# Third cross attention: the value product as two diagonal blocks of 64 columns

## The chip, the cores and the metric

The kernel runs on one core of a Trainium2 chip. The metric is device time in microseconds (us). A core has TensorE (in profile rows PE for matmuls, PEld for the loading of weights), VectorE (DVE), ScalarE (ACT), GpSimd (POOL) and SyncE (SP, which issues most DMAs). They meet through semaphores.

## The reference, cut to what matters

The model has twelve layers: four rounds of cross attention, self attention and a feed-forward layer, on 8 batches of 64 tokens with 256 channels. The change is in the third round's cross attention. It has 16 heads of 64 channels, 64 latents a batch, and 1601 context rows plus the 64 latents themselves as keys.

```python
xn, ln_lat = layer_norm(x, g1, b1), layer_norm(latents, g2, b2)
q = ln_lat @ Wq
k, v = jnp.split(jnp.concatenate([xn, ln_lat], axis=1) @ Wkv, 2, axis=-1)
...                                   # to 16 heads of 64
weight = softmax(mask(q * scale @ (k * scale).T))
out = einsum('bhln,bhnd->bhld', weight, v)
return out_as_rows @ Wout
```

## The kernel before, in words

`layer_2_xattn` (from line 3770) doesn't make keys and values of every head. It takes the key weights into the queries, and it weighs the normed context rows themselves: for each head the softmax weights times the rows give a mean row of 256 channels, and only that mean is multiplied with the head's value weights.

The work goes in 64 units: 8 batches (`b`) by 8 pairs of heads (`r`); u = 8 b + r. The 128 partitions of a unit are 2 heads of the pair by 64 latents. TensorE does for each unit, in `unit` (line 4040):

- `scores(u + 2)`, float16 products in three terms (line 4009), two units ahead of their use.
- sometimes a `prepare` group for a later batch (lines 3981, 3986, 3994).
- 13 products of the weights' high half with both halves of the rows, 512 columns each, into PSUM bank `ACC` (line 4055). Ahead of the one with m = 4 it calls `turn_means(u - 1)`, which transposes the mean rows of the unit before (line 4017).
- 13 products of the weights' low half with the rows' high half, 256 columns each (line 4060). Ahead of the one with m = 1 it calls `project(u - 1)`, the function that the change touches (line 4021).

`project` multiplies the pair's value weights `wv` (128 columns, 2 heads by 64 channels) with the turned means `meanT` (128 columns, 2 heads by 64 latents), in float32, summed over NC = 2 chunks of 128 channels, into bank 5. The result is 128 by 128: each head's value weights times each head's means. The two off-diagonal blocks mix one head's weights with the other's means. ScalarE's `keep_heads` (line 4160) takes only the diagonal ones, 64 by 64 each, to `oT`.

A float32 product appears in the records as two matmuls and two weight loads, so that the two calls in `project` are four records of each kind. The last unit's `project(63)` stands behind the loop, among the output products (line 4035).

Instructions stand in the order in which each engine's block issues them. TensorE's block takes waits on `post_read` (bank 5 is free) in `turn_means` and `project`. ScalarE turns meanT around between the two (`copy_means`).

Other places of the same kernel have products of 33 or 64 output columns, put to one of the two halves of the partitions: line 3431 (33 columns, first and last cross attention with heads of 16), line 912 (64 columns, 36 streamed), line 1284 (64 columns, 256 streamed, the halves in turn) and line 2789 (64 rows by 64 columns). Line 100 is `warm`, a full float16 product of 512 columns that holds no result.

Of the kernel before, what the change touches and what calls it, by code (L numbers as in the profile page):

```python
# [21 lines left out]
P = 128  # L22
B, S, D = 8, 64, 256
TOK = B * S
NT = TOK // P
NC = D // P
# [47 lines left out]
class Core:  # L74
# [19 lines left out]
    def sb(self, ctx, name, shape, dt=F32):  # L94
        return ctx.enter_context(self.nc.sbuf_tensor(name, shape, dt))
# [3674 lines left out]
def layer_2_xattn(k):  # L3770

    nc, PS, ins = k.nc, k.PS, k.ins
    DH = 64
# [12 lines left out]
    PREP, POST_BANK, ACC = (4, 6), 5, 7  # L3786
# [44 lines left out]
    with ExitStack() as c_:  # L3831
# [7 lines left out]
        wv = sb("wv", [P, NC, R * P])  # L3839
# [23 lines left out]
        meanT = sb("meanT", [P, NC, P])  # L3863
# [7 lines left out]
        with nc.Block() as block:  # L3871
# [100 lines left out]
            def _(pe):  # L3972
# [48 lines left out]
                def project(n):  # L4021
                    r = n % R
                    pe.wait_ge(post_read, 2 * n + 1)
                    for c in range(NC):
                        last = nc.tensor.matmul(PS[:, POST_BANK, 0:P], wv[:, c, r * P:(r + 1) * P], meanT[:, c, :],
                                                start=(c == 0), stop=(c == NC - 1))
                    last.then_inc(post_made, 1)

                def project_heads(t, heads):
# [10 lines left out]
                def unit(b, r):  # L4040
                    u = b * R + r
                    if u + 2 < U:
                        scores(u + 2)
                    for group, of in fills(b, r):
                        prepare(group, of)
                    if u == U - 2:
                        pe.wait_ge(prep_read, len(made_as))
                    if u + 2 >= U:
                        project_heads(u + 2 - U, range(R))
                    pe.wait_ge(high_turned, 16 * (u + 1))  # L4050
                    pe.wait_ge(sums_copied, u)
                    for m in range(KT):
                        if u > 0 and m == MEANS_AT:
                            turn_means(u - 1)
                        nc.tensor.matmul(PS[:, ACC, :], pth[:, u % 2, m, :], rows2[:, b % 2, :, :, m, :], start=(m == 0), stop=False)  # L4055
                    pe.wait_ge(low_turned, 16 * (u + 1))
                    for m in range(KT):
                        if u > 0 and m == VALUES_AT:
                            project(u - 1)
                        last = nc.tensor.matmul(PS[:, ACC, 0:D], ptl[:, u % 2, m, :], rows2[:, b % 2, 0, :, m, :], start=False,  # L4060
                                                stop=(m == KT - 1))
                    last.then_inc(sums_made, 1)
# [4 lines left out]
                for c in range(NC):  # L4067
                    last = nc.tensor.transpose(PS[:, FIRST_BANK, c * P:(c + 1) * P], lat[:, 0, c * P:(c + 1) * P], k.ident[:])
# [4 lines left out]
                for r in range(R):  # L4073
                    for j in range(NC):
                        last = nc.tensor.matmul(PS[:, Q_BANK, r * S:(r + 1) * S], wq[:, j, r * P:(r + 1) * P], latT[:, j, 0:S],
                                                start=(j == 0), stop=(j == NC - 1))
                last.then_inc(first_q, 1)
                pe.wait_ge(lat_scaled, NT)
                for c in range(NC):
                    for t in range(1, NT):  # L4080
                        last = nc.tensor.transpose(PS[:, LAT_BANK + c, t * P:(t + 1) * P], lat[:, t, c * P:(c + 1) * P], k.ident[:])
# [15 lines left out]
                pe.wait_ge(scored, U)  # L4097
                project_heads(3, range(R - 1))
                project(U - 1)
                project_heads(3, range(R - 1, R))  # L4100

# [355 lines left out]
```

## Time and profile before

| | |
|---|---|
| three runs, us | 2571.61 median, 2571.34 to 2571.94 |
| profiled execution, first to last instruction, us | 2561.7 |
| what lies around it, to the median of the runs, us | 9.9 |
| TensorE busy with matmuls | 2332.1 us, 91% |
| VectorE, ScalarE, GpSimd busy | 64%, 49%, 32% |

The profile has no total time of its own for the execution; the span from its first to its last instruction is compared with the median of the runs. A row of the timeline gives the start, and the time until the last of its records ends. Matmuls are pipelined: a record of 0.27 us does not hold TensorE for 0.27 us, and it is the distance between starts that counts. The shape `128*64 128x36 f32` is 128 rows and 64 columns of weights, 36 streamed columns in float32.

### The profile page before, as it was taken

To read this page: it belongs to the slowest core of one execution; us is meant where nothing else is said; L and a number is where in the kernel's file an instruction comes from. 1 tells how busy PE (TensorE), PEld (TensorE's weight loads), DVE (VectorE), ACT (ScalarE), POOL (GpSimd) and SP (SyncE) were. 2 spreads that over 40 slices of the span, in tenths; PEclk is the share of its full clock that TensorE was granted. 3 is DMA by queue.
4 is the path that set the end of the run, shared out by engine and by line. 5 is a ranking of instruction groups with operands and counts; after the bars stand their busy time and mean duration, and the time that the engine had idled before them with its cause. 6 is when DMAs were issued, how large, how long until landed. Compare 5 with 4: busy or idle time off the path is not lost. (4 is left out here: it accounts for less than half of the span.)

```text
span 2561.7 us, 44459 instructions
## 1 busy us (share of the span) xinstructions
PE 2332.1 (91%) x17354; PEld 1491.6 (58%) x17354; DVE 1651.5 (64%) x3198; ACT 1248.1 (49%) x2071; POOL 809.9 (32%) x660
## 2 busy tenths in 40 slices
PE   8885789999979889999999999699789999998898
PEld 6763556666654455656665666355456666666554
DVE  6976365555448756888888854654666666554577
ACT  3334145444444225555555553676345555554465
POOL 6610142242205202331233300055444454342253
PEclk9997899999999989999999999899999999999999
DMA  4202344233204047677776563133322222120221
GB/s 117 68 1 93 95 118 107 70 84 103 63 22 146 0 122 138 127 138 127 148 152 129 110 118 75 39 99 99 103 65 70 72 78 83 48 65 22 67 96 58
DMA packets 358593, 226.42 MB, mean 88 GB/s; under 512 B 289913, under 2 KB 326610, under 8 KB 358386
## 3 DMA queue, kind: packets, MB, share of 16 engines
q1 hardware_dynamic: 355314, 215.20, 34.5%
q0 software_dynamic: 3072, 8.39, 1.1%
q8 instruction: 139, 2.28, 0.4%
q14 instruction: 68, 0.56, 0.1%
HBM read 114.87 MB, written 0.52 MB: 45 GB/s over the span
## 5 line engine op out<-in xcount | busy, mean ns | idle before, releaser
L100 PE MATMUL PS<-hot 128*128 128x512 f16 x460 | 138.8, 439 | 82.4 <-DVE l0a_g L1119 17.5
L3951 POOL TENSOR_TENSOR l2x_rows<-l2x_rows,l2x_one 128x256 f16<-128x256 f32 (+1 forms) x91 | 90.9, 1025 | 378.9 <-DVE l2x_rows L1507 352.0
L4055 PE MATMUL PS<-l2x_rows,l2x_pth 128*128 128x512 f16 x832 | 200.4, 379 | 1.0 <-DVE l2x_mean L4264 0.9
L3709 DVE CUSTOM_DVE_ANT_0 l1x_junk<-PS,l1x_bias 128x1024 bf16<-128x1024 f32 (+1 forms) x128 | 123.3, 991 | 95.7 <-PE PS L3369 94.8
L4257 DVE TENSOR_TENSOR l2x_pl<-l2x_sc,l2x_ph 128x1664 f16<-128x1664 f32 x64 | 124.7, 1948 | 44.1 <-ACT l2x_ph L4134 43.4
L3709 DVE CUSTOM_DVE_ANT_0 l3x_junk<-PS,l3x_bias 128x1024 bf16<-128x1024 f32 (+1 forms) x128 | 123.6, 991 | 42.3 <-PE PS L3369 41.1
L4152 ACT ACTIVATE l2x_meanT<-PS 128x256 f32<-128x256 f32 x64 | 24.5, 383 | 250.0 <-PE PS L4017 250.0
L4242 DVE CUSTOM_DVE_ANT_0 l2x_sc<-PS,l2x_bias 128x1665 f32<-128x1665 f32 x64 | 120.9, 1889 | 38.2 <-issue 37.0
L3579 ACT ACTIVATE l3x_pT<-PS 128x512 f32<-128x512 f32 x144 | 84.5, 593 | 120.3 <-PE PS L3415 117.7
L100 PEld LDWEIGHTS PS<-hot 128*128 128x128 f16 x460 | 45.6, 109 | 154.0 <-issue 41.8
L4009 PE MATMUL PS<-l2x_kh,l2x_qth 128*128 128x512 f16 (+1 forms) x512 | 132.0, 339 | 1.5 <-issue 1.5
L4009 PE MATMUL PS<-l2x_kh,l2x_qtl 128*128 128x512 f16 (+1 forms) x512 | 132.0, 339 | 0.0
L4009 PE MATMUL PS<-l2x_kl,l2x_qth 128*128 128x512 f16 (+1 forms) x512 | 132.0, 339 | 0.0
L3579 ACT ACTIVATE l1x_pT<-PS 128x512 f32<-128x512 f32 x144 | 83.9, 594 | 88.3 <-PE PS L3415 87.8
L4055 PEld LDWEIGHTS PS<-l2x_rows,l2x_pth 128*128 128x128 f16 x832 | 79.3, 98 | 72.3 <-issue 2.6
L4127 ACT ACTIVATE l2x_sc<-l2x_sc,l2x_shift 128x1665 f32<-128x1665 f32 x64 | 107.9, 1686 | 19.5 <-DVE l2x_shift L4244 19.4
L4060 PE MATMUL PS<-l2x_rows,l2x_ptl 128*128 128x256 f16 x832 | 111.6, 273 | 0.0
L3431 PE MATMUL PS<-l1x_pT,l1x_v 128*33 128x128 f32 (+1 forms) x1664 | 110.9, 276 | 0.0
L3431 PE MATMUL PS<-l3x_pT,l3x_v 128*33 128x128 f32 (+1 forms) x1664 | 110.9, 276 | 0.0
L4134 ACT ACTIVATE l2x_ph<-l2x_sc 128x1664 f16<-128x1664 f32 x64 | 101.8, 1590 | 7.9 <-DMA l2x_pth<-l2x_ph 6.1
L3431 PEld LDWEIGHTS PS<-l3x_pT,l3x_v 128*33 128x33 f32 (+1 forms) x1664 | 83.4, 111 | 29.4 <-issue 20.1
L1642 POOL TENSOR_TENSOR l2f_unit_l<-l2f_unit,l2f_unit_h 128x384 f16<-128x384 f32 x72 | 74.6, 1058 | 70.9 <-ACT l2f_unit L1634 70.9
(867 smaller groups left out, 6231.0 us busy)
## 6 DMA issues: line engine op xcount, KB each, us to landing
l2f_unit<-in_L_ffn_units_dram SPq DMA_DIRECT2D x36, 384.0 KB, 3.0
l3f_unit<-in_L_ffn_units_dram SPq DMA_DIRECT2D x34, 384.0 KB, 2.9
l1x_kst<-l1x_kh SPq DMA_DIRECT2D x128, 100.1 KB, 2.2
l3x_kst<-l3x_kh SPq DMA_DIRECT2D x128, 100.1 KB, 2.2
l2x_rows<-in_ctx_dram SPq DMA_DIRECT2D x8, 1536.0 KB
l1x_ctx<-in_ctx_t_dram SPq DMA_DIRECT2D x7, 1601.0 KB, 7.3
l3x_ctx<-in_ctx_t_dram SPq DMA_DIRECT2D x7, 1601.0 KB, 6.6
l1x_kst<-l1x_kl SPq DMA_DIRECT2D x64, 100.1 KB, 2.2
```

The costliest lines, as they stand in the source:

```text
L100: self.nc.tensor.matmul(self.PS[:, bank, :], self.hot[:, 0:P], self.hot[:], start=True, stop=True)
L3431: last = nc.tensor.matmul(PS[at:at + VW, PV_BANK + b % 2, (u // 2) * P:(u // 2 + 1) * P], v33[0:n, b % 2, m, u, :], pT[0:n, (b * KT + m) % ...
L3579: nc.scalar.activation(to, of, ACT.Exp, scale=1.0 / S_SCALE).then_inc(exp_done, 1)
L3709: v.tensor_tensor_reduce(junk[:, slot(it), 0:n], slot_banks(it)[:, 0:n], bias[:, 0 if normed else b % 2, at:at + n], 1.0, LOWEST, ALU.add, ...
L3951: last = nc.gpsimd.tensor_tensor(high[:, at], of[:, at], one[0:p, at].unsqueeze(2).unsqueeze(3).to_broadcast([p, i, NC, P]), ALU.mult)
L4009: last = nc.tensor.matmul(PS[:, j, 0:n], x[:, d, r, :], y[:, b % 2, d, at:at + n], start=(e == 0), stop=(e == len(terms) - 1))
L4055: nc.tensor.matmul(PS[:, ACC, :], pth[:, u % 2, m, :], rows2[:, b % 2, :, :, m, :], start=(m == 0), stop=False)
L4060: last = nc.tensor.matmul(PS[:, ACC, 0:D], ptl[:, u % 2, m, :], rows2[:, b % 2, 0, :, m, :], start=False, stop=(m == KT - 1))
L4127: nc.scalar.activation(sc[:], sc[:], ACT.Exp, bias=shift[:, u % 2:u % 2 + 1], scale=1.0 / S_SCALE, accum_out=rsum[:, u % 4:u % 4 + 1]).the ...
L4134: nc.scalar.activation(ph[:], sc[:, 0:ODD], ACT.Copy).then_inc(p_high, 1)
L4242: link(v.tensor_tensor_reduce(sc[:], PS[:, 0:len(cols), :].rearrange("p b n -> p (b n)")[:, 0:KEYS], bias[:], 1.0, LOWEST, ALU.add, ALU.ma ...
L4257: v.tensor_tensor(pl[:], sc[:, 0:ODD], ph[:], ALU.subtract).then_inc(p_low, 1)
```

## The change

Each of the two full products of a unit (128 weight columns, 128 streamed columns) becomes two products of 64 weight columns and 64 streamed columns, one for each head. The first writes to partitions 0 to 63 and columns 0 to 63 of the bank, the second to partitions 64 to 127 and columns 64 to 127. The off-diagonal blocks are not computed, and nothing reads them. Waits, semaphore counts, buffers and all other engines' work stay as they are.

```diff
                     for c in range(NC):
-                        last = nc.tensor.matmul(PS[:, POST_BANK, 0:P], wv[:, c, r * P:(r + 1) * P], meanT[:, c, :],
-                                                start=(c == 0), stop=(c == NC - 1))
+                        for g in range(2):
+                            half = slice(g * S, (g + 1) * S)
+                            last = nc.tensor.matmul(PS[half, POST_BANK, half], wv[:, c, r * P + g * DH:r * P + (g + 1) * DH],
+                                                    meanT[:, c, half], start=(c == 0), stop=(c == NC - 1), skip_group_check=True)
                     last.then_inc(post_made, 1)
```

## Rows read from the trace of the kernel before

**Rows 1.** The page, its first lines (busy us, share of the span, instructions) and TensorE's granted clock in tenths.

```profile
span 2561.7 us, 44459 instructions
...
PE 2332.1 (91%) x17354; PEld 1491.6 (58%) x17354; DVE 1651.5 (64%) x3198; ACT 1248.1 (49%) x2071; POOL 809.9 (32%) x660
...
PEclk9997899999999989999999999899999999999999
```

**Rows 2.** The third cross attention's units (stretch, us, each engine's busy us, clock, DMA).

```profile
985.00:1592.00 607.00, 605.99 (x3759) 369.95 (x3758) 457.96 (x944) 317.11 (x549) 134.99 (x156) 1.00 0.66 127
```

**Rows 3.** TensorE's waits in that stretch; groups (busy, mean ns, idle); who waited for L4025.

```profile
PE PS L4055 <- DVE l2x_mean L4264: 0.9, 2, 0.7
...
L4060 PE MATMUL PS<-l2x_rows,l2x_ptl 128*128 128x256 f16 x832 | 111.6, 273 | 0.0
...
L4025 PE MATMUL PS<-l2x_meanT,l2x_wv 128*128 128x128 f32 x256 | 39.1, 275 | 0.0
...
  PE PS L4025: 7.3, 3
```

**Rows 4.** Timeline around one call of `project` (start us, us until the last record's end).

```profile
1105.83 0.27 PE L4060 MATMUL PS<-l2x_rows,l2x_ptl 128*128 128x256 f16 x1
...
1105.94 0.61 PE L4025 MATMUL PS<-l2x_meanT,l2x_wv 128*128 128x128 f32 x4
...
1106.38 0.38 PE L4060 MATMUL PS<-l2x_rows,l2x_ptl 128*128 128x256 f16 x2
```

**Rows 5.** The timeline where full products turn to 33-column ones and back.

```profile
2153.07 0.27 PE L3358 MATMUL PS<-l3x_wh,l3x_ctxl 128*128 128x256 f16 x1
...
2153.27 0.30 PE L3431 MATMUL PS<-l3x_pT,l3x_v 128*33 128x128 f32 x2
...
2153.27 0.41 PE L3431 MATMUL PS<-l3x_pT,l3x_v 128*33 128x128 f32 x3
...
505.11 1.07 PE L3431 MATMUL PS<-l1x_pT,l1x_v 128*33 128x128 f32 x16
...
2154.06 0.28 PE L3431 MATMUL PS<-l3x_pT,l3x_v 128*33 128x128 f32 x2
...
2154.27 0.39 PE L3412 MATMUL PS<-l3x_one_hot,l3x_fsp 128*128 128x512 f16 x1
```

**Rows 6.** The timeline of 64-column products in float32 with a full one between them.

```profile
218.45 1.12 PE L912 MATMUL PS<-l0a_v_out,l0a_a 128*64 128x36 f32 x16 [1.32 <-DVE l0a_v_out L1134]
...
219.50 0.39 PE L100 MATMUL PS<-hot 128*128 128x512 f16 x1
...
219.82 1.12 PE L912 MATMUL PS<-l0a_v_out,l0a_a 128*64 128x36 f32 x16
...
218.45 0.30 PE L912 MATMUL PS<-l0a_v_out,l0a_a 128*64 128x36 f32 x2 [1.32 <-DVE l0a_v_out L1134]
...
218.45 1.01 PEld L912 LDWEIGHTS PS<-l0a_v_out,l0a_a 128*64 128x64 f32 x16 [1.81 <-DVE l0a_v_out L1134]
...
L912 PEld LDWEIGHTS PS<-l0a_v_out,l0a_a x128: 132/138/139, 218.4 to 227.6; 128*64 128x64 f32 x128
...
L912 PE MATMUL PS<-l0a_v_out,l0a_a x128: 225/226/247, 218.4 to 227.7; 128*64 128x36 f32 x128
```

**Rows 7.** The timeline of 64-column products that go to the two halves in turn.

```profile
281.52 0.65 PE L1284 MATMUL PS<-l0f_w_down,l0f_mid 128*64 128x256 f32 x3 [0.74 <-ACT l0f_place L1350]
...
281.52 2.38 PE L1284 MATMUL PS<-l0f_w_down,l0f_mid 128*64 128x256 f32 x20 [0.74 <-ACT l0f_place L1350]
...
283.83 0.65 PE L1284 MATMUL PS<-l0f_w_down,l0f_mid 42*64 42x256 f32 x4
...
284.41 0.38 PE L1270 MATMUL PS<-l0f_xs,l0f_w_up 128*128 128x128 f32 x1
```

**Rows 8.** The timeline of 64 by 64 products in float16, two at a time.

```profile
2348.69 0.22 PE L2789 MATMUL PS<-l3a_kh,l3a_qh 64*64 64x64 f16 x2
...
2348.74 0.20 PE L2789 MATMUL PS<-l3a_kl,l3a_qh 64*64 64x64 f16 x2
```

## The prediction

> **What bounds the kernel now.** I read the page first: TensorE is busy 91% of a span of 2561.7 us, the next engine 64% [rows 1]. That is a mean over twelve layers, so the second view is the busy time of the stretch that the change touches. From 985 to 1592 us TensorE is busy 605.99 of 607.00 us at a granted clock of 1.00, the 2.4 GHz level [rows 2]. Third, the waits: in those 607 us TensorE waits 0.9 us for any other engine, and the groups at lines 4060 and 4025 have no idle time before them [rows 3]. So the stage is as long as TensorE's own sequence, and what `project` costs there, times 64, goes into the end. What hangs on its result is no path: ScalarE's copy to `oT` waited for line 4025 only 3 times, 7.3 us, and what it copies is read by the output products, which begin at unit 62 of 64 [rows 3]. The reader is to see that the only question is the distance from the last record ahead of `project` to the first behind it.
>
> **What it costs now.** The float16 record at 1105.83 us (line 4060, m = 0) is followed by four records of line 4025 and then by the next of line 4060 at 1106.38 us [rows 4]. That is 0.55 us: 0.11 for the 256 columns of the first, and four times 0.112 (a row of 0.61 us less one record of 0.275, over three) for the full products, 0.558 us by the sum. I take 0.555 us for the slot.
>
> **The change, part by part.** Four records of 128 by 128 go, eight of 64 by 64 come. The product's columns become a quarter (half streamed, and two can go at once), which is tempting. But products of 64 columns sit between full ones, and there the trace has a price at each border. I build the new slot from such rows.
>
> Into the halves: the full record of line 3358, 256 float16 columns as line 4060 has, starts at 2153.07 and the first 33-column one at 2153.27 us, 0.20 us later instead of 0.11 [rows 5]. The same with a 512-column record ahead: from 219.50 to 219.82, 0.32 us where 0.22 are two times the 0.11 of 256 columns [rows 6]. So TensorE lets the full product run out, about 0.095 us. 0.20 us.
>
> The first step: in line 3431 two records start together (two in 0.30 us, one taking almost all of that), and the third starts 0.41 - 0.27 = 0.14 us behind the first. Later pairs follow at (1.07 - 0.14 - 0.27) / 6 = 0.11 us [rows 5]. For 64 float32 columns of weights, line 1284: 0.65 - 0.38 = 0.27 us to the third record, later (2.38 - 0.38 - 0.27) / 8 = 0.216 us [rows 7]. The extra 0.05 us is the load of weights that nothing hides behind the border. 64 streamed columns should take half of what 128 do, 0.054 us. First step: 0.104 us.
>
> The further steps: with 36 streamed columns and 64 columns of weights, 14 steps take (1.12 - 0.226 - 0.078) / 14 = 0.058 us each, where 0.078 is the first (0.30 - 0.226, within the rounding), and the loads go at (1.01 - 0.138) / 15 = 0.058 us too [rows 6]. The load sets that pace, since 36 columns alone would take some 0.03 us. 0.058 against 0.054 for the stream: I take 0.058. Each half has four records (two chunks by two passes), so two more steps bring its last record: 0.116 us. That both halves go at once in float32 is the pair in rows 5 and the twenty records in 2.38 us of rows 7, ten steps and not twenty; that with 64 columns their loads keep up as well is the rows of line 2789, two records each 0.03 us in float16 with columns and rows halved [rows 8]. The second half starts 0.005 us behind the first.
>
> Out of the halves: the last pair of line 3431 starts at 2154.06 and 2154.07, the next full product at 2154.27 [rows 5]: 0.20 us, of which 0.11 stream, 0.09 to 0.10 are run-out. With 0.054 that gives 0.150 us. Line 912 gives it directly for a paced 64-column load: 218.45 + 1.12 - 0.226 = 219.344, next 219.50 [rows 6], 0.156 us. Line 1284 agrees: 283.83 + 0.65 - 0.38 = 284.10 to 284.41 us, 0.31 less the 0.216 of its stream [rows 7]. I take 0.153. The first full record behind a border is followed 0.01 us later than in a stream (the 0.32 us above against 0.22 + 0.09). 0.010 us.
>
> Sum: 0.200 + 0.104 + 0.116 + 0.005 + 0.153 + 0.010 = 0.588 us, against 0.555 us. That is 0.033 us more for each unit, and 64 of them make **+2.1 us**. The two borders cost 0.19 us and eat what the smaller products save. The span would go to 2563.8 us, and with the 9.9 us around it the time to 2573.7 us. Spacings to the rounding: with 0.054 for the steps, 0.147 for the way out, no 0.010 and 0.558 for the old slot it is +0.006 us a unit, +0.4 us; with 0.11, 0.060, 0.160, 0.015 and 0.550 it is +0.06 us, +4 us. The likeliest case's own range is 2572.0 to 2575.7 us.
>
> The Trainium skill says in TensorEngine Tiling (Array Packing), Key Properties, that a change of the tiling mode drains TensorE. By that rule the trace agrees: 0.09 to 0.10 us at each of the borders above. The page gives no price for it.
>
> What could hide the difference: nothing on TensorE, which doesn't idle here. The result is ready at about the same time, so `keep_heads`, `turn_means` and the `post_read` waits see no change. No DMA and no queue is touched. Behind the stage everything moves by the same amount. The last call, `project(63)`, stands among float32 products and is exposed; its borders are the same, and it counts as the 64th.
>
> **The rivals.**
>
> *No price at the borders (faster), 4 in 100.* If the accumulating float16 products of line 4060 and the halves could pass each other, 2 x 0.095 x 64 = 12.2 us come off: 2561.5 us. For it: only that no row has line 4060 itself at a border. Against it: each border in rows 5 to 7 shows 0.09 us or more.
> The Trainium skill's TensorEngine Tiling page, Theoretical Speedup, promises up to twice for each dimension of 64 or less. By that the four records' 0.45 us would be 0.11 us, and the time 2550 us; the page's own note on the drain and the rows speak against it, and this is held in the same 4 in 100.
>
> *The halves don't go side by side (slower), 6 in 100.* If the second half's records stand behind the first's, four more steps of 0.058 us come in: 0.232 x 64 = 14.8 us on top, 2588.5 us. It decides as soon as more than 0.05 us of a unit is added, that is with one of the four pairs apart. For it: in rows 5 and 7 the streams are 128 or 256 columns long, twice and more what the loads take, and rows 6 have one half only; the case of float32, 64 by 64 and both halves is nowhere. Against it: rows 8 pair loads and streams of equal length.
>
> *The load can't run under the stream (slower), 3 in 100.* Each step is then 0.05 + 0.054 us: 2 x 0.046 x 64 = 5.9 us more, 2579.6 us. Against it: the 0.058 us of rows 6 with loads that last 0.138 us.
> The Trainium skill's TensorE: Matmul & The Clock Gate, The mechanism, says that loads overlap matmuls in flight only when their row groups differ; here they are the same. By that this case would be the likely one. The steps in rows 6 have one row group and do overlap, and the measurement decides.
>
> *The change doesn't do what it says, 1 in 100.* The first half could be put as a full product with 64 columns in use; then there is a border between each two of four groups, 0.19 us more and serial steps: over 2595 us. Rows 7 show two records of such halves starting together, so hardly.
>
> *A later stage takes it up or adds to it, 6 in 100 beside the forecast.* A shift of some 2 us moves DMA and engine timings everywhere behind it. By half a step of a wait here and there this could be a few us to either side, 2567 to 2579 us; no row has such a wait in this stage.
>
> **How the numbers follow.** My case has 80 in 100. What a measurement of this kernel can tell from no change is 0.2%, 5.1 us: under 2566.5 or over 2576.7 us. My case is within it altogether. Faster: 4 for the free borders and 1 of the shifts, 5 in 100. Slower: 6 + 3 + 1, and 1 of the shifts and 1 for a sum at the top of all its bounds, 12 in 100. The same: 83 in 100. The predicted time is that of the case, 2573.7 us. The range takes the case's bounds and the nearer part of the shifts: 2570.8 to 2577.0 us; the cases outside it hold some 16 in 100.
>
> **What would show it.** The row of line 4025 doubles its records, with 64 by 64 shapes and two records starting together. From the start of line 4060's first record to that of its second it is 0.57 to 0.61 us instead of 0.55; 0.20 us to the first of line 4025, then 0.22 to the last, then 0.15 to 0.16. The weight loads show a gap with nothing to wait for at both borders, 128 of them. TensorE's busy time in the stage falls or stays by what its records cover, with the stage 2 us longer; the end of the stage moves from 1592 to about 1594 us. The forecast fails if the eight records take 0.45 us from first to last (the halves are serial), or if the border at line 4060 costs less than 0.05 us.

## The result and the profile after

The changed kernel took 2580.43 us (median of 14 executions, 2574.05 to 2584.95) against 2574.21 us of the kernel before (14 executions, 2570.42 to 2582.64). The ratio is 1.0023, 95% interval 1.0013 to 1.0034: 6 us slower, with 3 to 9 us in the interval. The forecast was 2.1 us slower, the same to within 0.2%, in a range that ends at 2577.0 us. Both are missed: the time is above the range, and the ratio is above 0.2%, though not clearly.

The page of the changed kernel, its span and busy times (those of before are in [rows 1]):

```profile
span 2572.5 us, 44924 instructions
...
PE 2319.3 (90%) x17563; PEld 1471.3 (57%) x17610; DVE 1652.2 (64%) x3198; ACT 1247.8 (49%) x2071; POOL 806.0 (31%) x660
```

The span is 10.8 us longer than that in [rows 1], but most of this is no work of the change. The next rows give the stage by its first product of the low half and its last output product; they say, for each line, count, ns min/median/max, and the first and last start. First the kernel before, profiled twice (the second time in the run e1_same below, another execution of the same text, not taken side by side with the first), then the changed kernel.

```profile
L4060 PE MATMUL PS<-l2x_rows,l2x_ptl x832: 272/273/273, 974.9 to 1585.0; 128*128 128x256 f16 x167
...
L4035 PE MATMUL PS<-l2x_wo,l2x_oT x64: 378/379/482, 1568.0 to 1593.3; 128*128 128x256 f32 x64
```

```profile
L4060 PE MATMUL PS<-l2x_rows,l2x_ptl x832: 272/273/273, 987.4 to 1597.5; 128*128 128x256 f16 x167
...
L4035 PE MATMUL PS<-l2x_wo,l2x_oT x64: 379/379/483, 1580.6 to 1605.8; 128*128 128x256 f32 x64
```

```profile
L4062 PE MATMUL PS<-l2x_rows,l2x_ptl x832: 272/273/283, 981.7 to 1596.0; 128*128 128x256 f16 x167
...
L4037 PE MATMUL PS<-l2x_wo,l2x_oT x64: 379/379/483, 1579.0 to 1604.2; 128*128 128x256 f32 x64
```

The unchanged kernel comes to this stage at 974.9 us in one execution and at 987.4 us in the other, 12.5 us apart, and then takes 1593.3 - 974.9 = 618.4 us and 1605.8 - 987.4 = 618.4 us for it. The changed kernel comes at 981.7 us and takes 1604.2 - 981.7 = 622.5 us. So whole executions differ by many microseconds ahead of the change, while the stage of the kernel before repeats to 0.1 us. Behind the stage nothing is added: the rest of the span is 968.4 us before and 968.3 us after. I call the 618.4 and 622.5 us the stage's length and read every run by it; it comes from two rounded starts, so a difference of two lengths is good to 0.2 us. In this trace the change costs **4.1 us** there.

TensorE's timeline around one `project`, matmuls and then weight loads (compare [rows 4]), and all of line 4027 (count, ns; then where weight loads sat idle):

```profile
1113.93 0.27 PE L4062 MATMUL PS<-l2x_rows,l2x_ptl 128*128 128x256 f16 x1
...
1114.13 0.45 PE L4027 MATMUL PS<-l2x_meanT,l2x_wv 128*64 128x64 f32 x8
...
1114.52 0.28 PE L4062 MATMUL PS<-l2x_rows,l2x_ptl 128*128 128x256 f16 x1
```

```profile
1114.13 0.31 PEld L4027 LDWEIGHTS PS<-l2x_meanT,l2x_wv 128*64 128x64 f32 x8 [0.32 <-issue]
...
1114.51 0.33 PEld L4062 LDWEIGHTS PS<-l2x_rows,l2x_ptl 128*128 128x128 f16 x4
```

```profile
L4027 PE MATMUL PS<-l2x_meanT,l2x_wv x512: 222/222/271, 993.0 to 1603.1; 128*64 128x64 f32 x171
...
  issue: 20.3, 64
```

There are 512 records where there were 256. From the float16 record at 1113.93 it is 0.20 us to the first 64-column one, and 0.59 us to the next float16 one, for 0.55 us in [rows 4]. Eight records end 0.45 us after the first starts; less the 0.22 us of one, their starts span 0.23 us. The weight loads sit idle for 0.32 us at each entry, 64 times, with nothing to wait for: TensorE finishes the full product before it starts on the halves. This is the picture that was forecast. What wasn't is this wait, TensorE's longest in the stage (us in all, times, longest; [rows 3] has 0.9 us in two waits for the kernel before):

```profile
PE PS L4057 <- DVE l2x_mean L4266: 2.7, 5, 0.8
```

It stands mostly in the third unit of a batch. There the kernel before and the changed one differ like this, in the second batch (timeline; in each fence SyncE's issue of the context rows, the first of the two transposes of softmax weights behind it, and ScalarE's copy `ph` of the unit after; in the second also TensorE's product that then had to wait):

```profile
1068.52 0.38 SPq L1467 DMA_DIRECT2D l2x_rows<-in_ctx_dram  x1
...
1070.33 4.62 SPq L3902 DMA_TRANSPOSE l2x_pth<-l2x_ph  x1
...
1077.85 1.59 ACT L4134 ACTIVATE l2x_ph<-l2x_sc 128x1664 f16<-128x1664 f32 x1 [0.79 <-DMA l2x_pth<-l2x_ph]
```

```profile
1075.52 0.39 SPq L1467 DMA_DIRECT2D l2x_rows<-in_ctx_dram  x1
...
1077.35 4.74 SPq L3902 DMA_TRANSPOSE l2x_pth<-l2x_ph  x1
...
1086.45 1.59 ACT L4136 ACTIVATE l2x_ph<-l2x_sc 128x1664 f16<-128x1664 f32 x1 [2.33 <-DMA l2x_pth<-l2x_ph]
...
1091.34 1.02 PE L4057 MATMUL PS<-l2x_rows,l2x_pth 128*128 128x512 f16 x4 [0.77 <-DVE l2x_mean L4266]
```

SyncE issues a batch of context rows, 1.5 MB, at 1068.5 us in the kernel before and at 1075.5 us in the changed one, and behind it two transposes of softmax weights. In the first the copy `ph` begins 9.3 us after that issue (1077.85), in the second 10.9 us (1086.45), having waited 2.33 us for the first transpose to land and not 0.79. VectorE's mean comes later, and TensorE waits 0.77 us at line 4057.

What moved on the DMA queues 8.0 to 9.2 us behind that issue differs too (packets, MB, share; first the kernel before, then the changed one):

```profile
q1 hardware_dynamic: 1377, 0.34, 127.6%
```

```profile
q1 hardware_dynamic: 738, 0.19, 202.6%
...
q8 instruction: 1, 0.02, 5.2%
```

In the changed kernel one packet of instructions, 16 KB, falls into the transposes, and in the same 1.2 us the queue of the transposes gets through 738 packets and not 1377. What this packet has to do with the change stands under "The step that failed".

### The profile page after: what moved, and what is told of

It is laid out like the page before. It is cut to its first block and busy times, and to the rows that moved or that the text cites. A ratio compares the mean times of both kernels' runs of the same rounds, so it can differ in the third digit from the quotient of the medians.

```text
span 2572.5 us, 44924 instructions
## 1 busy us (share of the span) xinstructions
PE 2319.3 (90%) x17563; PEld 1471.3 (57%) x17610; DVE 1652.2 (64%) x3198; ACT 1247.8 (49%) x2071; POOL 806.0 (31%) x660
## 5 line engine op out<-in xcount | busy, mean ns | idle before, releaser
L100 PE MATMUL PS<-hot 128*128 128x512 f16 x460 | 133.1, 425 | 82.1 <-DVE l0a_g L1119 17.5
L4136 ACT ACTIVATE l2x_ph<-l2x_sc 128x1664 f16<-128x1664 f32 x64 | 101.8, 1591 | 11.1 <-DMA l2x_pth<-l2x_ph 9.2
```

Source lines behind the costliest of these rows:

```text
L100: self.nc.tensor.matmul(self.PS[:, bank, :], self.hot[:, 0:P], self.hot[:], start=True, stop=True)
L4136: nc.scalar.activation(ph[:], sc[:, 0:ODD], ACT.Copy).then_inc(p_high, 1)
```

## The experiments

All ratios below are of device times against the kernel before on the same chip; the stage's length is read as above, from the two rows of each run's own trace, one trace for each run.

| run | ratio, 95% interval | stage, us | to before, us |
|---|---|---|---|
| before | | 618.4 | |
| e1_same | 0.9997, 0.9984 to 1.0010 | 618.4 | 0.0 |
| changed kernel | 1.0023, 1.0013 to 1.0034 | 622.5 | +4.1 |
| e2_after | 1.0012, 0.9999 to 1.0026 | 621.4 | +3.0 |
| e3_split | 1.0063, 1.0046 to 1.0081 | 635.5 | +17.1 |
| e4_group4 | 0.9986, 0.9975 to 0.9997 | 613.1 | -5.3 |
| e5_delay | 1.0027, 1.0016 to 1.0038 | 624.5 | +6.1 |
| e6_group4b | 0.9995, 0.9985 to 1.0005 | 616.1 | -2.3 |
| e7_weights_half | 1.0064, 1.0046 to 1.0082 | 632.3 | +13.9 |
| e8_half_by_half | one time | 621.9 | +3.5 |
| e9_before_moved | 0.9997, 0.9987 to 1.0006 | 617.2 | -1.2 |
| e10_after_moved | 1.0004, 0.9995 to 1.0014 | 619.4 | +1.0 |
| e11_group4_moved | 0.9973, 0.9962 to 0.9984 | 611.1 | -7.3 |
| e12_group4b_moved | 0.9968, 0.9956 to 0.9980 | 608.5 | -9.9 |

**e1_same.** No edit.

> The kernel before, unchanged, against itself. It measures what a comparison of this kernel shows when nothing differs. Theory A (the change costs 0.042 us for each of 64 units, 2.7 us, and the rest of the measured 6.2 us is scatter between executions of layers ahead of the change): the two sides differ by up to 0.15% and their interval is about as wide as the change's own; the stage of the third cross attention lasts the same to within 2 us from execution to execution, and the first layer differs by several us. Theory B (the change costs 6 us, by something beyond the slot on TensorE): the two sides agree within 0.05%.

The interval of a kernel against itself is 0.26% wide, and 5 us of difference are at the edge of what such a comparison sees. The stage is the same to 0.1 us. The scatter of theory A is there, ahead of the stage: 974.9 and 987.4 us. Part of it may be the chip: the kernel before has a median of 2577.25 us here and 2561.79 us on the chip of e5_delay to e8_half_by_half.

**e2_after.** The changed kernel again.

> The changed kernel once more. Theory A: ratio 1.001 (+2.7 us), interval reaching to 1.000; each slot 587 ns, each unit 42 ns longer than before. Theory B: ratio 1.0023 again, with the stage 4 to 6 us longer than the stage of the kernel before.

Ratio 1.0012, and the stage 3.0 us longer. Theory A's slots are right (0.587 us, as above), but the 4.1 and 3.0 us of the two traces are more than the slots give, so it isn't whole; theory B's 6 us aren't in the stage either. The two traces of the changed kernel are 1.1 us apart, so its stage repeats less well than that of the kernel before.

**e3_split.** A dose of borders: the first chunk of 128 channels in one slot, the second in another, two products later.

```diff
                         if u > 0 and m == VALUES_AT:
-                            project(u - 1)
+                            project(u - 1, [0])
+                        if u > 0 and m == VALUES_AT + 2:
+                            project(u - 1, [1])
```

> The changed kernel with the second chunk's four 64-column products ahead of the float16 product m = 3, and the first chunk's where they were: one more border into the halves and one more out of them for each of 63 units, no other work. Each slot should be 0.203 + 0.110 + 0.154 us, and 0.011 for the record behind it. Theory A (borders cost what the rows show): two slots of 0.467 us in place of one of 0.587 and one plain step of 0.109, with 0.011 more behind the second, 0.25 us a unit, +16 us against the changed kernel, +18.5 us against the kernel before, ratio 1.007. Rival (the borders are shown in the records but hidden in the total, and the load of 64 columns is the price): under +5 us against the changed kernel.

```profile
1117.18 0.27 PE L4065 MATMUL PS<-l2x_rows,l2x_ptl 128*128 128x256 f16 x1
...
1117.39 0.34 PE L4027 MATMUL PS<-l2x_meanT,l2x_wv 128*64 128x64 f32 x4
...
1117.65 0.39 PE L4065 MATMUL PS<-l2x_rows,l2x_ptl 128*128 128x256 f16 x2
...
1117.98 0.34 PE L4027 MATMUL PS<-l2x_meanT,l2x_wv 128*64 128x64 f32 x4
```

The same eight records in two slots. From 1117.18 to 1117.65 us the first slot lasts 0.47 us, of which the four records' starts span 0.34 - 0.22 = 0.12 us. The rest, 0.35 us, is two borders and the float16 record's own columns. The stage is 13.0 us longer than in the changed kernel's first trace and 14.1 us longer than in its second; 16 were expected. Each plain unit did grow by 0.25 us, and the rest is the changed kernel's long third units, which this one hardly has. The rival, under 5 us, falls.

**e4_group4.** One slot for four units. ScalarE's copies go to four buffers (`GROUP` is 4), and the products of four units go out behind the last. The last four units go as two, one and one.

```diff
-        meanT = sb("meanT", [P, NC, P])
+        meanT = sb("meanT", [P, GROUP, NC, P])
...
                 def project(n):
-                    r = n % R
+                    if n != group_of[n][-1]:
+                        return
...
+                    for i, m in enumerate(group_of[n]):
+                        r = m % R
...
+                                last = nc.tensor.matmul(PS[half, POST_BANK, D + i * S:D + (i + 1) * S], ...
```

> The changed kernel with the 64-column products of four units together: the turned means wait in four buffers, and the products of the four units go out in one slot, to 256 columns of the same bank. Borders for 18 slots and not for 64. Theory A: a slot of 0.203 + 0.104 + 14 x 0.058 + 0.005 + 0.154 + 0.011 = 1.29 us for four units and three plain steps of 0.109, against 4 x 0.556 before: 0.15 us less a unit, -9.5 us against the kernel before, ratio 0.996 to 0.997. Rival (something else than the borders makes the change slow, such as the weights' loads or the number of instructions): no faster than the kernel before.

```profile
1110.63 0.27 PE L4076 MATMUL PS<-l2x_rows,l2x_ptl 128*128 128x256 f16 x1
...
1110.83 1.15 PE L4040 MATMUL PS<-l2x_meanT,l2x_wv 128*64 128x64 f32 x32
...
1111.92 0.50 PE L4076 MATMUL PS<-l2x_rows,l2x_ptl 128*128 128x256 f16 x3
```

Thirty-two records in a slot of 1.29 us; the expectation's 1.29 us hold 0.011 for the record behind the slot, so this is 0.01 us more. The gain in the stage is 5.3 us of 9.5. TensorE's waits in the whole stage say where the rest went (us in all, times, longest), and the kernel is faster than before by 0.14%:

```profile
PE PS L4071 <- DVE l2x_mean L4283: 4.1, 10, 0.9
```

Three of the ten waits are in third units of a batch, six of 0.31 to 0.32 us at the crossing from one batch to the next, and one of 0.65 us in unit 61.

**e5_delay.** The full products of before, each unit made late in another way.

```diff
+                    nc.tensor.matmul(PS[:, POST_BANK, 384:384 + 98], k.hot[:, 0:P], k.hot[:, 0:98], start=True, stop=True)
                     for c in range(NC):
                         last = nc.tensor.matmul(PS[:, POST_BANK, 0:P], wv[:, c, r * P:(r + 1) * P], meanT[:, c, :],
```

> The kernel before, with its full products, and ahead of them in each unit one more full float16 product of 98 streamed columns, 0.041 us, into columns of the bank that nothing reads: no border, but the same lateness for each unit as the 64-column blocks bring. Theory A1 (the changed kernel's stage is 3 to 4 us longer because each unit is 0.041 us late, 2.0 us after what slack takes up, and because a late TensorE meets the context rows' transfer otherwise, 1 to 2 us of waits at line 4055 in the third unit of a batch): the slot lasts 0.597 us, the stage is 3 to 4 us longer than before, and the same units (11, 19, 27) are 0.4 to 1 us longer. Theory A2 (the waits come of the 64-column form itself or of its many instructions): the stage is 2.0 us longer, with no new waits.

```profile
1095.51 0.27 PE L4061 MATMUL PS<-l2x_rows,l2x_ptl 128*128 128x256 f16 x1
...
1095.62 0.21 PE L4024 MATMUL PS<-hot 128*128 128x98 f16 x1
...
1095.66 0.68 PE L4026 MATMUL PS<-l2x_meanT,l2x_wv 128*128 128x128 f32 x4
...
1096.17 0.49 PE L4061 MATMUL PS<-l2x_rows,l2x_ptl 128*128 128x256 f16 x3
```

The slot is 0.66 us, not 0.597: 98 columns stream in 0.04 us, but the second of the float32 records starts 0.18 us behind the first and not 0.11. That is 0.22 us behind the start of their weight loads, as in the kernel before, so it looks like a wait for its 128 columns of weights; no run varies this alone. The row of four lasts 0.68 us where it lasts 0.61 in [rows 4]. So the dose was 0.109 us a unit and not 0.041, 6.9 us in all, and the stage grew by 6.1. One third unit was long, in the first of the three batches, and the other two weren't. That is neither theory's number: a long third unit needs no border and no 64-column form, but making every unit late, here by 2.6 times as much, isn't enough to make three of them.

**e6_group4b.** e4_group4 with other groups.

```diff
-    groups = [list(range(i, min(i + GROUP, U - 2))) for i in range(0, U - 2, GROUP)] + [[U - 2], [U - 1]]
+    groups = [[0, 1, 2]] + [list(range(i, i + GROUP)) for i in range(3, U - 1, GROUP)] + [[U - 1]]
```

> Four units' 64-column products together as in e4_group4, with the groups moved by one unit, so that every second slot falls into the unit that crosses from one batch to the next, where e4_group4 got nothing back for its three spared slots (9.147 us before and after): there VectorE's chain sets the pace and TensorE has 0.45 us of slack. Theory (the second bound takes it up): seven slots are hidden by 0.45 us each, 3 us off e4_group4, and 8 us off the kernel before, ratio 0.997. Rival (the slack is not at that place but in TensorE's own order): as e4_group4, -3.6 to -5 us.

```profile
PE PS L4071 <- DVE l2x_mean L4285: 7.5, 6, 1.7
```

It gains 2.3 us on the kernel before, less than e4_group4. TensorE waits 7.5 us, in six places, up to 1.7 us each. The expectation saw one second bound and not the other: the third units' transposes.

**e7_weights_half.** Half of the change: 64 weight columns, but 128 streamed.

```diff
-                            last = nc.tensor.matmul(PS[half, POST_BANK, half], wv[...],
-                                                    meanT[:, c, half], ...
+                            last = nc.tensor.matmul(PS[half, POST_BANK, 0:P], wv[...],
+                                                    meanT[:, c, :], ...
```

> Half of the change alone: 64 weight columns to one half of the partitions, but all 128 streamed columns, so that the off-diagonal blocks are computed again. Theory (steps are the longer of stream and load, halves side by side, borders 0.095 us each): 0.203 + 0.158 + 2 x 0.108 + 0.007 + 0.205 us = 0.79 us for a slot against 0.587 in the changed kernel and 0.556 before, and 0.011 behind it: 0.245 us more a unit than before, +15 us, ratio 1.006. Rival (the borders alone make the price, and the stream is hidden): as the changed kernel, +3 us.

```profile
1100.87 0.27 PE L4062 MATMUL PS<-l2x_rows,l2x_ptl 128*128 128x256 f16 x1
...
1101.07 0.66 PE L4027 MATMUL PS<-l2x_meanT,l2x_wv 128*64 128x128 f32 x8
...
1101.66 0.39 PE L4062 MATMUL PS<-l2x_rows,l2x_ptl 128*128 128x256 f16 x2
```

The slot is 0.79 us. With 128 streamed columns a step takes 0.107 us, as the stream does; with 64 it takes 0.058 us, the same as with 36 in [rows 6], so there the load sets it. The stage is 13.9 us longer, 15 were expected, and no third unit is long.

**e8_half_by_half.** The order of the four products.

```diff
-                    for c in range(NC):
-                        for g in range(2):
+                    for g in range(2):
+                        for c in range(NC):
```

> The changed kernel with the order of its four products changed: both chunks of the first half, then both of the second. Theory (TensorE takes the halves side by side from a short look ahead in the order of issue): the second half's four records begin up to three records behind the first's, and first to last record is 0.26 to 0.35 us in place of 0.230, the unit 0.03 to 0.12 us longer than in the changed kernel. Rival 1 (each half has its own order, whatever the distance): 0.230 us as before. Rival 2 (only records next to each other can go together): 0.45 us, 0.22 us a unit, +14 us.

```profile
1097.81 0.27 PE L4062 MATMUL PS<-l2x_rows,l2x_ptl 128*128 128x256 f16 x1
...
1098.02 0.46 PE L4027 MATMUL PS<-l2x_meanT,l2x_wv 128*64 128x64 f32 x8
...
1098.41 0.39 PE L4062 MATMUL PS<-l2x_rows,l2x_ptl 128*128 128x256 f16 x2
```

The row of eight is 0.46 us long where it is 0.45 in the changed kernel. Both halves still go at once with four records of one half issued ahead of the other's: rival 1 is right at a distance of four records, and TensorE doesn't need neighbours to take them together. A longer distance was not tried. The stage rests on this one execution.

**e9_before_moved and e10_after_moved.** The transfer of the context rows behind the unit's transposes, in both kernels, and VectorE's sums over those rows out of the third unit of each batch.

```diff
-                        if b + 2 < B and r == 1:
-                            src.load(sp, b + 2)
...
                         if u + 2 < U:
                             turn(u + 2)
+                        if b + 2 < B and r == 1:
+                            src.load(sp, b + 2)
...
-                        if r in (2, 3, 4, 5):
-                            src.moments(dve, link, x, range(4 * (r - 2), min(4 * (r - 1), KT + 1)))
+                        if r in (3, 4, 5):
+                            src.moments(dve, link, x, range(5 * (r - 3), min(5 * (r - 2), KT + 1)))
```

> The kernel before with the transfer of the context rows of the batch after next issued behind the transposes of that unit, not ahead of them, and VectorE's sums over those rows made one unit later, in three units and not four. In ten traces the third unit of a batch came out in two ways: ScalarE's copy to the high half could begin 11.5 or 13.1 us into the second unit, by when the transposes behind the 1.5 MB transfer had landed, and in the later case the unit is 0.4 to 1 us longer. Theory A3 (these late landings are the part of the change's price that its slot on TensorE doesn't explain): with the transfer moved no batch has the long third unit, and the stage is 1 us shorter than before. Rival (the transposes are late for another reason): the long units stay.

> The changed kernel with the same transfer moved. Theory A3: its stage is longer than that of e9_before_moved by the slots alone, 2.0 to 2.7 us, where it was 3.1 and 4.2 us with the transfer in its old place. Rival (the change costs more by itself): 3 to 4 us longer again.

TensorE's wait for the mean, and the rows of the stage's ends, e9_before_moved first:

```profile
PE PS L4055 <- DVE l2x_mean L4264: 0.2, 1, 0.2
...
L4060 PE MATMUL PS<-l2x_rows,l2x_ptl x832: 272/273/273, 991.5 to 1600.4; 128*128 128x256 f16 x167
...
L4035 PE MATMUL PS<-l2x_wo,l2x_oT x64: 379/379/483, 1583.5 to 1608.7; 128*128 128x256 f32 x64
```

```profile
PE PS L4057 <- DVE l2x_mean L4266: 0.2, 1, 0.2
...
L4062 PE MATMUL PS<-l2x_rows,l2x_ptl x832: 272/273/283, 984.0 to 1595.1; 128*128 128x256 f16 x167
...
L4037 PE MATMUL PS<-l2x_wo,l2x_oT x64: 379/379/483, 1578.2 to 1603.4; 128*128 128x256 f32 x64
```

Both kernels now wait 0.2 us, where they waited 0.9 and 2.7. The stages are 617.2 and 619.4 us: 2.2 us between them, in the 2.0 to 2.7 of theory A3, where it was 4.1 and 3.0. The 0.2 us are left in unit 61, and no third unit is long. The edit moves two things, the transfer and VectorE's sums, and no run moves one alone. For the transfer speaks that ScalarE's copy in the second unit no longer waits for a transpose (0.03 us idle before it, where it had 0.6 to 2.3), and that in the unmoved kernels, where every batch has the same sums, only some batches are long.

**e11_group4_moved and e12_group4b_moved.** The same move in e4_group4 and e6_group4b.

> e4_group4 with the same transfer moved. Its slots alone give 15 x 0.60 = 9.0 us back and it kept 5.2 us, with 4 us of that lost in long third units and at the batch borders. Theory A3: the third units' loss of 1.8 us and more comes back; the stage is 7 to 8 us shorter than before, and the ratio to the kernel before 0.997. Rival: as e4_group4.

> e6_group4b with the same transfer moved. Theory: in e6_group4b the slots at the batch borders were hidden by 0.45 us, as expected, and the third units took more than that back (7.5 us of waits). With the transfer moved both gains stand: 9 to 10 us off the kernel before, ratio 0.996. Rival (VectorE's chain sets the pace in more units than those): no faster than e11_group4_moved.

```profile
PE PS L4071 <- DVE l2x_mean L4285: 0.6, 1, 0.6
...
L4076 PE MATMUL PS<-l2x_rows,l2x_ptl x832: 272/273/283, 991.4 to 1591.7; 128*128 128x256 f16 x167
...
L4051 PE MATMUL PS<-l2x_wo,l2x_oT x64: 379/379/483, 1574.0 to 1599.9; 128*128 128x256 f32 x64
```

Of 7.5 us of waits 0.6 are left, and the stage is 9.9 us shorter than before. e12_group4b_moved beats the kernel before at a ratio of 0.9968 (0.9956 to 0.9980), and its stage is 14.0 us shorter than the changed kernel's. e11_group4_moved takes 7.3 us off. Seven waits are left in it, the six at the batch borders and the one in unit 61:

```profile
PE PS L4071 <- DVE l2x_mean L4283: 2.5, 7, 0.6
```

The 2.6 us between the two kernels are the slots at the batch borders, which e6_group4b was made for.

## Why the prediction was wrong

**What bounds the kernel.** Right in the main and wrong in one sentence. The distance between the two float16 records around `project` does set the price. But [rows 3] has 0.9 us of TensorE waiting for VectorE's mean at line 4055, and I passed over it as nothing. 0.7 us of it, one long third unit in the sixth batch, was what could be seen of a second chain, the transposes behind the context rows' transfer, that runs so close behind TensorE that the same kernel has it long in some batches and short in others.

**The slot, term by term.** Way in 0.203 us (0.200 forecast), first to last record 0.230 (0.225), way out 0.154 (0.153), and the next record 0.011 later (0.010). In all the new slot and the record behind it add 0.042 us a unit, not 0.033, each term of the forecast being up to 5 ns short. Of 64 x 0.042 = 2.7 us the stage keeps 2.2, the difference of e10_after_moved and e9_before_moved: where a batch ends and the next begins, VectorE's chain sets the pace. The timeline of TensorE has the first low-half record of the last two units of a batch; the distance between the two is one unit. First the kernel before, then e4_group4, which has no slot there:

```profile
1047.92 0.27 PE L4060 MATMUL PS<-l2x_rows,l2x_ptl 128*128 128x256 f16 x1
...
1057.07 0.27 PE L4060 MATMUL PS<-l2x_rows,l2x_ptl 128*128 128x256 f16 x1
```

```profile
1062.35 0.38 PE L4076 MATMUL PS<-l2x_rows,l2x_ptl 128*128 128x256 f16 x2
...
1071.50 0.27 PE L4076 MATMUL PS<-l2x_rows,l2x_ptl 128*128 128x256 f16 x1
```

9.15 us before, 9.16 in the changed kernel (1054.91 to 1064.07), and still 9.15 with the whole slot gone. TensorE can save nothing there, and of the 0.042 us that the change adds only some 0.01 comes through.

**The step that failed** is "nothing on TensorE, which doesn't idle here [...] No DMA and no queue is touched". Against the kernel before, the third units of the second, third and fourth batch are 0.93, 0.41 and 0.78 us longer in the first trace of the changed kernel beyond the 0.042 (0.77, 0.38 and 0.63 in the second; e8_half_by_half has the same three). The sixth batch's is long in both traces of the kernel before, and in one of the two of the changed kernel. This is worth 4.1 - 2.2 = 1.9 us in one trace and 3.0 - 2.2 = 0.8 us in the other. With the transfer and the sums moved no third unit is long in either kernel.

A queue is touched after all, that of the instructions. Ten traces have the transfer in its old place, and in each the second to sixth batch can be read, 50 cases. In 24 a 16 KB packet of instructions on queue 8 starts 8.0 to 8.9 us behind the issue of the transfer, and the first transpose lands 10.5 to 11.1 us behind it. In 25 of the other 26 it lands at 9.0 to 9.7 us (the last, in e3_split, at 10.5). The packets come 31 times in the units of the kernel before and 33 times in the changed one's, once per some 250 matmul and weight-load records of TensorE, and the change adds 504 such records. So it shifts the places where they fall: in the kernel before the sixth batch has one among its transposes, in the changed one the second, third and fourth do; in e5_delay, with full products, none does, and its one long unit goes with a packet at 10.4 us, behind which the second transpose landed late. A late landing is not enough for a long unit: e7_weights_half has three and no long one, its units being 0.25 us longer. Nor is it always needed: in the changed kernel's first trace the sixth batch's landed on time, but the transfer was issued at least 1.2 us later in its unit than in the other batches. No run moves the packets by themselves, so that the packet is what holds the transpose up stays argued from this agreement.

**The total.** By the stage the change costs 3 to 4 us, 0.12 to 0.16%. The measured 0.23% has this at or just under the low end of its interval, and the second comparison gave 0.12%. The kernel against itself leaves 0.13% to either side. So the forecast "the same within 0.2%" was near for the change, and the absolute time wasn't. It was 2573.7 us, the measured 2580.4. Of these 6.7 us, 2.6 are the kernel before, whose 14 executions have a median of 2574.2 and not the 2571.6 of the three that I had. They span 12 us where the three spanned 0.6, and the range of 6 us stood on those. The other 4.1 us are the measured difference of 6.2 less the 2.1 forecast: by the traces 1 to 2 are in the stage, and the rest shows neither there nor behind it and is no more than the scatter ahead of it. The traces of all runs come to the stage at 972.6 to 992.9 us of the span.

**The rivals.** No price at the borders: wrong, e3_split. The halves one behind the other: wrong, eight starts in 0.23 us. The load not under the stream: wrong by the same. The first half as a full product: wrong, there is one entry and one way out. A later stage taking it up or adding to it: wrong, it was this stage that added.

The Trainium skill's rule on draining (TensorEngine Tiling (Array Packing), Key Properties) holds at 126 borders more, 0.203 us on the way in where a plain step takes 0.109. The Trainium skill's "up to 2x" for each small dimension (TensorEngine Tiling (Array Packing), Theoretical Speedup) did not come: 0.23 us between first and last start where it was 0.335, and a border on each side. What the Trainium skill says of loads and row groups (TensorE: Matmul & The Clock Gate, The mechanism) isn't what these float32 products of one row group do: they take steps of 0.058 us with loads of 0.138. In both the measurement decides.

## What to carry to other kernels

Where a few small column-tiled products stand in a stream of full ones, count the borders first: here two of 0.1 us undid a halving of the products, and collecting four units' products into one slot turned the same edit from a loss to a gain. An engine that is busy 99.8% of a stage can still have a second chain at its heels; a wait of 0.9 us in 607 was the sign of it, and before such a chain is moved or given slack, neither a saving nor a cost on the first engine arrives whole. An edit that adds only TensorE instructions can shift when instruction packets travel among other transfers; the queues of the profile show it. Judge changes under 0.3% by the length of the stage in the traces, and check on the unchanged kernel how well that repeats.

## What the runs showed that I had not expected

The two halves go at once even when the order of issue has all four records of one ahead of the other's: 0.46 us for the row of eight and not 0.45 (e8_half_by_half). A float16 product of 98 columns ahead of the float32 ones cost 0.109 us for 0.041 us of columns (e5_delay). And executions of one kernel came to the same place in the program 12.5 us apart, while the 618.4 us behind it agreed to 0.1 us.
